# A decoder layer on one core: ScalarE multiplies the probabilities of 22 head pairs with the reciprocal sums, row by row, in place of VectorE and GpSimd

## The chip, the cores and the metric

The kernel runs on one core of a Trainium2 chip. A core has five engines with queues of their own: TensorE (PE, matrix products; its weight loads are shown as PEld), VectorE (DVE), ScalarE (ACT), GpSimd (POOL) and SyncE (SP, which here only issues transfers). They meet at semaphores alone: an instruction waits until a counter has reached a value, and all that stands behind it in its engine's queue waits too. The metric is the device time of one execution in microseconds.

## The reference

One pre-norm decoder layer in float32 over x of 16 sequences x 128 tokens x 256 features, three blocks, each on a layer norm of x and added to x:

- attention with 16 heads of 128: Q, K, V = x̂ W + b; rotary embedding of Q and K; scores Q K^T / sqrt(128), causal mask; `probs = softmax(scores)`; `z = probs V`; `out = z W_O + b_O`. This is the block that the change touches: of the softmax it is the division by the row sum.
- a long convolution of 256 features with filters of 128 taps, gated by a context (`ctx_2048`).
- a mixture of experts, 16 experts of 176 with the best 4 a token, beside a shared expert of 704.

## The kernel before

**Tiling.** The 16 sequences are four groups (g = 0 to 3) of GB = 4, a group being 512 tokens. The 16 heads are PAIRS = 8 pairs. The attention is a loop over steps s = 8g + p, one for each pair p of a group, and three more to drain it. All five engines run this loop, each with its own order written out by hand. Step s works on several pairs at once: Q and K of pair p (of number s), V, scores, maxima and exponentials of number s - 1, the weighed values of number s - 2, and the output projection of number s - 3. `live(k)` says whether the pair k back exists. Weights are kept as two float32r parts (`_hi`, `_lo`), and a product is three matmuls (lines 594 to 596, 656 to 658).

**What runs beside the attention.** From g = 1 on, the steps also carry the convolution block of the group before: at p = 2 its layer norm (`cross_head`, line 1657), at p = 3 turned tokens and a skip term (`vcs`, `cross_skip`), from p = 4 on products `kv` on GpSimd (line 1475), matmuls with them on TensorE (lines 713 to 715) and multiplications and sums on VectorE (lines 1684, 1699). For g = 2 and 3 the routing of the group two back stands there as well: at p = 2 TensorE turns its tokens (`token_turn`, line 609), which ScalarE and VectorE split (`tokens_high`, `th`; `tl`).

**A pair's softmax.** For head h of the pair VectorE scales and masks the scores into `prob[h]` (line 1600) and takes the negated row maximum (1604). ScalarE takes the exponential, one ACTIVATE for each of the four sequences, with the row sum from its accumulator (1226). VectorE takes the reciprocal `rtotal` (1608). A multiplication of `prob[h]` by `rtotal` follows: for h = 0 on GpSimd (`first_probs`, 1412), for h = 1 on VectorE (`second_probs`, 1628), one instruction of 128 x 512 with the reciprocals broadcast.

**Two ways to turn the probabilities.** z needs them transposed. For pairs 8 to 29 (`by_dma`, 22 of 32) ScalarE copies `prob[h]` into two planes of 16-bit halves (`prob_planes`, 1214), SP stores them in DRAM (489) and a transposing DMA brings them back as `prob_t[h]` (494). The other pairs are transposed by TensorE (669). Then TensorE weighs the values (687), ScalarE adds the bias of V (`take_weighed`, 1259) and rounds to `z_hi` (1266), GpSimd makes `z_lo` (1407), and TensorE projects (892 to 896) one step later.

**What sets the order around the change.** ScalarE's step begins with the two halves of V (`take_values`, 1237, `v_taken`), which TensorE has projected into bank 1 and bank 4, then the planes of head 1; then, for each head, exponential, bias, `z_hi`; last the planes of head 0. TensorE uses bank 1 again once V has been taken from it: at p = 0 for the second half of the turned tokens of the next group (865), at p = 2 (g = 2 and 3) for `token_turn` right behind V's projection, otherwise behind the output projection. VectorE's step ends with four `turn` products of Q and K (1619) with the two reciprocals among them, then `second_probs`, then `rot` (1640) of Q and K; GpSimd does the other half of `rot` (1447). TensorE's scores (919) need all four.

Of the kernel before, what the change touches and what calls it, by code (L numbers as in the profile page):

```python
# [8 lines left out]
ACT = mybir.ActivationFunctionType  # L9
# [5 lines left out]
GB = 4  # L15
# [57 lines left out]
def by_dma(t):  # L73
    return PAIRS <= t < PAIRS * GROUPS - 2


def dma_before(t):
    return min(max(t - PAIRS, 0), PAIRS * (GROUPS - 1) - 2)
# [24 lines left out]
def decoder(nc, x_in, wqkv_in, bqk_in, bv_in, wo_in, bo_in, trig_in, mask_in, ident_in,  # L103
# [7 lines left out]
    with ExitStack() as ctx:  # L111
        def sb(name, shape, dt=F32, c=ctx):
            return c.enter_context(nc.sbuf_tensor(name, shape, dt))
# [4 lines left out]
        def sem(name):  # L118
            return ctx.enter_context(nc.semaphore(name))
# [67 lines left out]
        prob = [sb(f"prob{h}", [128, GB, SEQ], c=tctx) for h in range(2)]  # L187
# [11 lines left out]
        rtotal = sb("rtotal", [128, 2, GB], c=tctx)  # L199
# [110 lines left out]
        rtotal_ready = sem("rtotal_ready")  # L310
        prob_ready = [sem(f"prob_ready{h}") for h in range(2)]
# [88 lines left out]
        def value_order(g, p, live):  # L400
            late = live(1) and live(2) and (p in (1, 2) or (g == 0 and p > 2)) and not by_dma(g * PAIRS + p - 2)
            return (1, 0) if late else (0, 1)
# [735 lines left out]
        def _(act):  # L1138
            def split_hi(n):
                act.wait_ge(raw_loaded[n % 2], 16 * (n // 2 + 1))  # L1140
                p = n // CH
                if p >= WRING and n % CH == 0:
                    act.wait_ge(w_stored[W_AT[p]], 64 * W_NTH[p])
                    act.wait_ge(v_ready, 2 * (p - WRING) + 2)
                nc.scalar.copy(w_hi[:, W_AT[p], n % CH, :], raw[n % 2][:]).then_inc(w_hi_done, 1)
# [18 lines left out]
            def root(lo, hi):  # L1164
                k = roots[0]
                roots[0] += 1
                act.wait_ge(var_ready, 2 * k + 2)
                nc.scalar.activation(rstd[:, lo:hi], newton[:, lo:hi], ACT.Sqrt).then_inc(rstd_ready, 1)
# [41 lines left out]
            def prob_planes(t, h):  # L1210
                act.wait_ge(prob_ready[h], t + 1)
                if dma_before(t):
                    act.wait_ge(prob_stored, 16 * (2 * dma_before(t) + h - 1))
                nc.scalar.copy(planes[h][:], prob[h][:].bitcast(U16).rearrange("p b (k i) -> p b i k", i=2)).then_inc(planes_ready, 1)

            root(0, GB)
            split_hi(0)
            split_hi(1)

            def step(g, p, live, first):  # L1220
                s = g * PAIRS + p
# [9 lines left out]
                order = value_order(g, p, live)  # L1231

                def take_values(half):
                    act.wait_ge(v_ready, s * 2 - 1 + order.index(half))
                    if live(3):
                        act.wait_ge(zt_ready, s * 2 - 4)
                    nc.scalar.copy(v[(p - 1) % 2][:, 2 * half:2 * half + 2, :],
                                   v_bank[half][:].rearrange("p (b n) -> p b n", b=2)).then_inc(v_taken, 1)

                if live(1):  # L1240
                    take_values(order[0])
                    if order == (0, 1):
                        take_values(1)
                if by_dma(s - 2):
                    prob_planes(s - 2, 1)
                if p == 0 and live(0):
                    for c in range(CH):
                        act.wait_ge(xt_ready, g * 2 + c + 1)
                        nc.scalar.copy(xt_hi[:, c, :], proj[c][:]).then_inc(xt_hi_done, 1)
# [25 lines left out]
                elif live(2):  # L1275
                    for i in range(4):
                        h = i % 2
# [26 lines left out]
                if live(1) and not by_dma(s - 2):  # L1304
                    exps(0)
                    exps(1)
                if by_dma(s - 1):
                    prob_planes(s - 1, 0)
                if first and p < PAIRS - 1:
                    split_hi(2 * p + 2)  # L1310
# [6 lines left out]
                if p == 2 and 0 < g < GROUPS:  # L1317
                    root((g - 1) * GB, g * GB)

            attention(step)  # L1320


# [79 lines left out]
        def _(pool):  # L1402
# [7 lines left out]
            def first_probs(s):  # L1410
                pool.wait_ge(rtotal_ready, s * 2 - 1)
                nc.gpsimd.tensor_tensor(prob[0][:], prob[0][:],  # L1412
                                        rtotal[:, 0, :].unsqueeze(2).to_broadcast([128, GB, SEQ]),
                                        ALU.mult).then_inc(prob_ready[0], 1)
                pool.wait_ge(prob_ready[0], s)

            def core_step(g, p, live, first):
                s = g * PAIRS + p
                late = by_dma(s - 2)
                if live(2):  # L1420
                    z_low(s, 0)
                    if not late:
                        z_low(s, 1)
                if late:
                    first_probs(s)
                    z_low(s, 1)
                for m in range(2):
                    if live(0):
                        pool.wait_ge(qk_used, s * 4 + 2 * m + 2)
                        if live(1):  # L1430
                            pool.wait_ge(s_ready, s * 2)
                        pool_rot(m, s)
                    if m == 0 and live(1) and not late:
                        first_probs(s)
                if p == 1 and live(0):

                    pool.wait_ge(small_loaded, SMALL)
                    pool.wait_ge(xhat_ready, g * GB + GB)
                    xg = x[:, g * GB:(g + 1) * GB, :]
                    nc.gpsimd.tensor_tensor(xg, xg, bo[:].unsqueeze(1).to_broadcast([128, GB, D]),  # L1440
                                            ALU.add).then_inc(bo_added, 1)
                    pool.wait_ge(bo_added, g + 1)
# [46 lines left out]
            last = GROUPS - 1  # L1489
# [21 lines left out]
        def _(dve):  # L1511
# [61 lines left out]
            def step(g, p, live, first):  # L1573
                s = g * PAIRS + p
# [35 lines left out]
                for m in range(2):  # L1610
                    t = turn[m]
                    if live(0):
                        for i in range(2):

                            dve.wait_ge(qk_ready, s * 4 + 2 * m + i + 1)
                            if i == 0 and live(1):
                                dve.wait_ge(rot_pool, s * 2 - 1 + m)
                                dve.wait_ge(rot_dve, s * 2 - 1 + m)
                            last = nc.vector.scalar_tensor_tensor(  # L1619
                                turn_all[m][:, 2 * i:2 * i + 2, :], qk_bank[2 * m + i][:].unsqueeze(1).to_broadcast([128, 2, GT]),  # L1620
                                bqk[:, p, 2 * m + i:2 * m + i + 1],
                                trig[:].rearrange("p a b t -> p a (b t)"), ALU.add, ALU.mult)
# [3 lines left out]
                def second_probs():  # L1626
                    dve.wait_ge(rtotal_ready, s * 2)
                    nc.vector.tensor_tensor(prob[1][:], prob[1][:],
                                            rtotal[:, 1, :].unsqueeze(2).to_broadcast([128, GB, SEQ]),
                                            ALU.mult).then_inc(prob_ready[1], 1)  # L1630

                if by_dma(s - 1):
                    second_probs()
                for m in range(2):
                    t = turn[m]
                    if live(0):
# [316 lines left out]
            last = GROUPS - 1  # L1953
# [222 lines left out]
```

## Time and profile before

| | us |
|---|---|
| median of three runs | 947.0 (946.83 to 950.6) |
| the profiled execution, its own time | 949.05 |
| its span, from first to last instruction | 947.2 |
| TensorE busy | 900.5 (95%) |
| VectorE busy | 801.2 (85%) |
| ScalarE busy | 455.7 (48%) |
| GpSimd busy | 498.5 (53%) |

A row of waits names who waited, for whom, the total, how often and the longest. A row of a timeline has start and duration, engine, line, operation, output and input tiles, how many were merged, and in brackets the idle time before it and who ended it. Matmuls overlap, so the durations of neighbours don't add. PEclk is TensorE's granted clock as a share of full speed.

### The profile page before, as it was taken

The numbers are of one execution on the slowest core, as the hardware profiler recorded it, in microseconds if no ns is written. First come the engines' busy times: TensorE is split into PE (matmuls) and PEld (weight loads), VectorE is DVE, ScalarE is ACT, GpSimd is POOL, SyncE is SP. The second block draws the span as 40 slices with busy tenths as digits, with TensorE's granted clock in tenths as the row PEclk, the third lists the DMA queues.
The fourth block names the chain that finished last, engine by engine and source line by source line (L and its number), as shares of the span: only waits on it lengthen the run. The fifth ranks groups of instructions, "written<-read, shape, count | busy, mean of one in ns | idle before, by whom it ended". The sixth has DMA issues, their size and how long they took to land.

```text
span 947.2 us, 19251 instructions
## 1 busy us (share of the span) xinstructions
PE 900.5 (95%) x6119; PEld 803.3 (85%) x6119; DVE 801.2 (85%) x1706; ACT 455.7 (48%) x1227; POOL 498.5 (53%) x380
## 2 busy tenths in 40 slices
PE   7899999999999989999998999989998999999996
PEld 6798888888899878898897888877887799999985
DVE  7988877988888989888897988966788888888867
ACT  3657655554445554444664433562155344445430
POOL 1533434465563435777362677625717377777760
PEclk9999999999999999999998999999999999999998
DMA  8795381665445654655788666425255377787879
GB/s 279 274 352 215 129 308 48 177 183 197 134 143 167 212 171 134 186 172 182 225 266 270 206 197 182 138 84 217 72 199 165 79 131 128 128 132 127 130 123 302
DMA packets 137489, 169.59 MB, mean 179 GB/s; under 512 B 54960, under 2 KB 112176, under 8 KB 136112
## 3 DMA queue, kind: packets, MB, share of 16 engines
q1 hardware_dynamic: 122944, 149.31, 48.9%
q0 software_dynamic: 14448, 19.05, 12.4%
q8 instruction: 53, 0.87, 0.4%
q14 instruction: 44, 0.36, 0.1%
HBM read 100.52 MB, written 58.44 MB: 168 GB/s over the span
## 4 chain that ended last, share of the span: by engine, by line
PE 68%; DVE 15%; issue 6%; POOL 5%; DMA 3%; ACT 2%; SPq 1%; DVEq 0%; POOLq 0%
PE bank L656 5%; PE bank L658 5%; PE bank L657 5%; PE bank L687 5%; PE bank L919 5%; PE bank L594 5%; PE bank L596 4%; PE bank L595 4%; PE bank L1032 4%; DVE rot L1640 3%; PE bank L713 3%; DVE turn L1619 3%; PE bank L714 3%; PE bank L715 3%; POOL xs L1454 2%
## 5 line engine op out<-in xcount | busy, mean ns | idle before, releaser
L1619 DVE SCALAR_TENSOR_TENSOR turn<-bank,bqk,trig 128x1024 f32<-128x1024 f32 x128 | 162.4, 1279 | 30.9 <-PE bank L658 28.9
L1407 POOL TENSOR_TENSOR z_lo<-prob_t,z_hi 128x512 fp32r<-128x512 f32 x64 | 83.5, 1304 | 199.0 <-ACT z_hi L1266 197.9
L1226 ACT ACTIVATE prob<-prob,negmax 128x128 f32<-128x128 f32 x256 | 99.4, 390 | 124.2 <-DVE negmax L1604 124.1
L1506 POOL DMA_INDIRECT sums<-ysb,token_at x79 | 123.3, 1560 | 56.8 <-DMA sums<-ysb,token_at 28.2
L1447 POOL TENSOR_TENSOR rot<-turn 128x512 f32<-128x512 f32 x64 | 95.4, 1490 | 42.5 <-DVE turn L1619 30.3
L656 PE MATMUL bank<-xt_hi,w_hi 128*128 128x512 f32 x256 | 109.6, 428 | 6.2 <-DVE vcs L1674 4.1
L658 PE MATMUL bank<-xt_hi,w_lo 128*128 128x512 f32 x256 | 101.9, 398 | 0.0
L657 PE MATMUL bank<-xt_lo,w_hi 128*128 128x512 f32 x256 | 101.4, 396 | 0.0
L1454 POOL DMA_INDIRECT xs<-xh,dest x64 | 71.4, 1115 | 43.0 <-DVE dest L1787 25.2
L1640 DVE TENSOR_TENSOR rot<-turn 128x512 f32<-128x512 f32 x64 | 93.0, 1493 | 0.0
L1475 POOL TENSOR_TENSOR kv<-c_t,v_t 128x512 f32<-128x512 f32 x60 | 71.8, 1224 | 19.2 <-ACT v_t L1188 12.2
L687 PEld LDWEIGHTS bank<-prob_t,v 128*128 128x128 f32 x512 | 66.2, 193 | 13.1 <-issue 6.3
L892 PE MATMUL bank<-wo_hi,z_hi 128*128 128x256 f32 x256 | 73.7, 288 | 3.6 <-issue 3.6
L594 PE MATMUL bank<-w_hi,xt_hi 128*128 128x256 f32 x256 | 73.6, 288 | 2.2 <-DVE turn L1619 2.1
L687 PE MATMUL bank<-prob_t,v 128*128 128x128 f32 x512 | 68.5, 277 | 6.6 <-ACT prob_t L1259 4.2
L894 PE MATMUL bank<-wo_lo,z_hi 128*128 128x256 f32 x256 | 73.1, 285 | 0.0
L896 PE MATMUL bank<-wo_hi,z_lo 128*128 128x256 f32 x256 | 73.1, 285 | 0.0
L596 PE MATMUL bank<-w_hi,xt_lo 128*128 128x256 f32 x256 | 72.4, 283 | 0.0
L595 PE MATMUL bank<-w_lo,xt_hi 128*128 128x256 f32 x256 | 72.4, 283 | 0.0
L919 PE MATMUL bank<-rot 64*128 64x128 f32 x1024 | 65.8, 278 | 2.6 <-DVE rot L1640 2.6
L919 PEld LDWEIGHTS bank<-rot 64*128 64x128 f32 x1024 | 59.6, 188 | 9.9 <-issue 5.6
L1412 POOL TENSOR_TENSOR prob<-prob,rtotal 128x512 f32<-128x512 f32 x32 | 33.3, 1041 | 59.2 <-DVE rtotal L1608 58.5
(202 smaller groups left out, 2563.7 us busy)
## 6 DMA issues: line engine op xcount, KB each, us to landing
w_hi<-w_dram SPq DMA_DIRECT2D x24, 768.0 KB, 5.1
w_lo<-w_dram SPq DMA_DIRECT2D x24, 768.0 KB, 6.3
prob_dram<-planes SPq DMA_DIRECT2D x44, 256.0 KB, 2.4
xe_all<-xs SPq DMA_DIRECT2D x79, 132.5 KB, 2.7
wo_hi<-wo_dram SPq DMA_DIRECT2D x26, 256.0 KB, 6.5
wo_lo<-wo_dram SPq DMA_DIRECT2D x26, 256.0 KB, 7.2
sums<-zeros SPq DMA_DIRECT2D x3, 2176.0 KB, 13.1
raw<-in_wqkv SPq DMA_DIRECT2D x16, 384.0 KB, 4.4
```

What stands on the lines that cost most here:

```text
L594: nc.tensor.matmul(o, lh, rh, start=(i == 0), stop=False)
L595: nc.tensor.matmul(o, lh, rl, start=False, stop=False)
L596: last = nc.tensor.matmul(o, ll, rh, start=False, stop=(i == n - 1))
L656: nc.tensor.matmul(o, hi, xt_hi[:, c, :], start=(c == 0), stop=False)
L657: nc.tensor.matmul(o, hi, xt_lo[:, c, :], start=False, stop=False)
L658: last = nc.tensor.matmul(o, lo, xt_hi[:, c, :], start=False, stop=(c == CH - 1))
L687: last = nc.tensor.matmul(zt_bank[:, b * 128:(b + 1) * 128], v[p % 2][:, b, h * DH:(h + 1) * DH], prob_t[h][:, b, :], start=True, stop=True)
L919: last = nc.tensor.matmul(score[h][:, t], rot[0][i][rows, t], rot[1][i][rows, t], start=(i == 0), stop=(i == 1))
L1226: last = nc.scalar.activation(prob[h][:, b, :], prob[h][:, b, :], ACT.Exp, bias=negmax[:, h, b:b + 1], accum_out=total[:, h, b:b + 1])
L1506: nc.gpsimd.indirect_dma_start(sums_dram[s % SUMS], bass.IndirectOffsetOnAxis(ap=token_at[:, s:s + 1], axis=0), ysb[s % YBUFS][:], None, c ...
L1619: last = nc.vector.scalar_tensor_tensor(turn_all[m][:, 2 * i:2 * i + 2, :], qk_bank[2 * m + i][:].unsqueeze(1).to_broadcast([128, 2, GT]), ...
L1640: nc.vector.tensor_tensor(rot[m][0][:], t[0], t[3], ALU.subtract).then_inc(rot_dve, 1)
```

## The change

In steps whose pair goes by DMA, ScalarE gets `weigh_probs(t, h)`: it waits for the reciprocal of pair t and head h and multiplies `prob[h]` in place, one ACTIVATE of 128 x 128 for each of the four sequences, the reciprocal of a row as its per-partition scale. For head 1 it stands at the start of the step after next, ahead of V's halves; for head 0 at the end of the next step, ahead of its planes. `second_probs` and `first_probs` are no longer called for these pairs. At the step's start the order on ScalarE becomes: product of head 1, V of bank 1, planes of head 1, V of bank 4 (before: both halves of V, then the planes). The other ten pairs are as before. Lines behind 1215 move by 7 to 10.

```diff
+            def weigh_probs(t, h):
+                act.wait_ge(rtotal_ready, 2 * t + h + 1)
+                for b in range(GB):
+                    last = nc.scalar.activation(prob[h][:, b, :], prob[h][:, b, :], ACT.Copy,
+                                                scale=rtotal[:, h, b:b + 1])
+                last.then_inc(prob_ready[h], 1)
...
+                if by_dma(s - 2):
+                    weigh_probs(s - 2, 1)
                 if live(1):
                     take_values(order[0])
-                    if order == (0, 1):
-                        take_values(1)
                 if by_dma(s - 2):
                     prob_planes(s - 2, 1)
+                if live(1) and order == (0, 1):
+                    take_values(1)
...
                 if by_dma(s - 1):
+                    weigh_probs(s - 1, 0)
                     prob_planes(s - 1, 0)
...
                 if late:
-                    first_probs(s)
+                    if not by_dma(s - 1):
+                        first_probs(s)
                     z_low(s, 1)
...
-                    if m == 0 and live(1) and not late:
+                    if m == 0 and live(1) and not late and not by_dma(s - 1):
                         first_probs(s)
...
-                if by_dma(s - 1):
-                    second_probs()
```

ScalarE's queue where step 17 (g = 2, p = 1) ends and step 18 begins, before; `bank1` and `bank4` hold the projected V:

```order
L1266 CAST z_hi1<-prob_t1 128x512
L1214 COPY planes0<-prob0 128x1024
L1237 COPY v1<-bank1 128x512
L1237 COPY v1<-bank4 128x512
L1214 COPY planes1<-prob1 128x1024
```

The same place after; `th_early` is the copy of the routed tokens that TensorE turned:

```order
L1275 CAST z_hi1<-prob_t1 128x512
L1219 ACTIVATE prob0<-prob0,rtotal 128x128 x4
L1214 COPY planes0<-prob0 128x1024
L1219 ACTIVATE prob1<-prob1,rtotal 128x128 x4
L1244 COPY v1<-bank1 128x512
L1214 COPY planes1<-prob1 128x1024
L1244 COPY v1<-bank4 128x512
L1201 CAST th_early<-bank0 128x512
```

Four ACTIVATEs now stand ahead of the planes of head 0 and four ahead of V of bank 1, and V of bank 4 has moved behind the planes of head 1.

GpSimd's queue in a step with `kv` products, before:

```order
L1407 TENSOR_TENSOR z_lo0<-prob_t0,z_hi0 128x512
L1412 TENSOR_TENSOR prob0<-prob0,rtotal 128x512
L1407 TENSOR_TENSOR z_lo1<-prob_t1,z_hi1 128x512
L1447 TENSOR_TENSOR rot01<-turn0 128x512
L1447 TENSOR_TENSOR rot11<-turn1 128x512
L1475 TENSOR_TENSOR kv0<-c_t,v_t 128x512
```

And after:

```order
L1417 TENSOR_TENSOR z_lo0<-prob_t0,z_hi0 128x512
L1417 TENSOR_TENSOR z_lo1<-prob_t1,z_hi1 128x512
L1458 TENSOR_TENSOR rot01<-turn0 128x512
L1458 TENSOR_TENSOR rot11<-turn1 128x512
L1486 TENSOR_TENSOR kv0<-c_t,v_t 128x512
```

The product, with its wait for the reciprocal, is gone from between the two `z_lo`. VectorE's queue loses line 1628 between the last reciprocal and `rot` in the same way; TensorE's and SP's queues are unchanged.

## Rows read from the trace of the kernel before

**Rows 1.** The page, engine busy us (share of the span) xinstructions

```profile
PE 900.5 (95%) x6119; PEld 803.3 (85%) x6119; DVE 801.2 (85%) x1706; ACT 455.7 (48%) x1227; POOL 498.5 (53%) x380
```

**Rows 2.** Waits of TensorE, 156:606: us in total, times, longest

```profile
PE bank L656 <- DVE vcs L1674: 4.1, 2, 3.1
PE bank L687 <- ACT prob_t L1259: 2.5, 2, 1.7
PE bank L687 <- DMA prob_t<-prob_dram: 2.4, 2, 1.8
PE bank L713 <- POOL kv L1475: 1.9, 3, 0.8
PE bank L919 <- DVE rot L1640: 1.4, 2, 0.9
PE bank L703 <- DVE vcs L1669: 0.8, 3, 0.3
PE bank L713 <- DVE zc L1684: 0.4, 1, 0.4
```

**Rows 3.** Groups, 160:592: shapes xcount | busy us, mean ns | idle before

```profile
L1226 ACT ACTIVATE prob<-prob,negmax 128x128 f32<-128x128 f32 x176 | 68.4, 390 | 121.7 <-DVE negmax L1604 121.7
...
L1628 DVE TENSOR_TENSOR prob<-prob,rtotal 128x512 f32<-128x512 f32 x22 | 34.8, 1581 | 0.7
...
L1259 ACT ACTIVATE prob_t<-bank,bv 128x512 f32<-128x512 f32 x42 | 28.5, 677 | 26.4 <-PE bank L687 26.3
...
L1412 POOL TENSOR_TENSOR prob<-prob,rtotal 128x512 f32<-128x512 f32 x22 | 22.9, 1041 | 52.3 <-DVE rtotal L1608 52.2
```

**Rows 4.** Timeline of VectorE, 334 to 341: start us, us, operation

```profile
335.30 1.80 DVE L1628 TENSOR_TENSOR prob<-prob,rtotal 128x512 f32<-128x512 f32 x1
337.02 2.38 DVE L1640 TENSOR_TENSOR rot<-turn 128x512 f32<-128x512 f32 x2
```

**Rows 5.** Timeline of GpSimd, 331 to 341 us

```profile
334.00 1.30 POOL L1407 TENSOR_TENSOR z_lo<-prob_t,z_hi 128x512 fp32r<-128x512 f32 x1 [0.66 <-ACT z_hi L1266]
335.25 3.01 POOL L1447 TENSOR_TENSOR rot<-turn 128x512 f32<-128x512 f32 x2
```

**Rows 6.** Timeline of ScalarE, 316 to 321.5 us

```profile
316.13 0.62 ACT L1266 CAST z_hi<-prob_t 128x512 fp32r<-128x512 f32 x1
316.66 1.04 ACT L1214 COPY planes<-prob 128x1024 uint16<-128x1024 uint16 x1
317.61 0.58 ACT L1237 COPY v<-bank 128x512 f32<-128x512 f32 x1
```

**Rows 7.** Timeline of ScalarE, 419 to 426 us

```profile
420.70 1.05 ACT L1214 COPY planes<-prob 128x1024 uint16<-128x1024 uint16 x1 [2.56 <-POOL prob L1412]
422.33 0.59 ACT L1237 COPY v<-bank 128x512 f32<-128x512 f32 x1 [0.58 <-PE bank L596]
...
424.26 1.05 ACT L1214 COPY planes<-prob 128x1024 uint16<-128x1024 uint16 x1
```

**Rows 8.** Timeline of TensorE, 426 to 427.5 us

```profile
426.64 0.67 PE L713 MATMUL bank<-kv,toep 128*128 128x256 f32 x2
```

**Rows 9.** Timeline of VectorE at 317 and at 422 us, line 1608

```profile
317.23 0.17 DVE L1608 RECIPROCAL rtotal<-total 128x4 f32<-128x4 f32 x1
...
422.10 0.17 DVE L1608 RECIPROCAL rtotal<-total 128x4 f32<-128x4 f32 x1
```

**Rows 10.** Timeline of TensorE, 318.6 to 320 us

```profile
318.70 1.03 PE L609 MATMUL bank<-ident,xh 128*128 128x128 f32 x8
```

**Rows 11.** Timeline of ScalarE and TensorE, 283 to 286 us

```profile
283.14 0.59 ACT L1237 COPY v<-bank 128x512 f32<-128x512 f32 x1 [0.58 <-PE bank L596]
...
284.38 1.04 PE L865 MATMUL bank<-ident,xhat 128*128 128x128 f32 x8
```

**Rows 12.** Windows: busy us of each engine, PEclk, DMA share, GB/s

```profile
313.50:318.70 5.20, 5.20 (x38) 4.93 (x39) 5.16 (x8) 4.65 (x13) 4.09 (x4) 1.00 0.32 121
...
351.50:354.90 3.40, 3.40 (x11) 2.68 (x10) 1.45 (x3) 0.70 (x4) 1.62 (x2) 0.51 0.02 7
```

## The prediction

> **What bounds the kernel now.** I read the busy table first [rows 1]: TensorE is busy 900.5 of 947.2 us. The change touches steps 9 to 31 (step s = 8g + p), about 160 to 606 us. A busy TensorE row is no proof that it sets the end, so I read next what TensorE waited for in this stretch [rows 2]. The seven sums make 4.1 + 2.5 + 2.4 + 1.9 + 1.4 + 0.8 + 0.4 = 13.5 us in 450. That is the prize: 4.1 + 1.4 + 0.8 + 0.4 = 6.7 us end with VectorE, 1.9 with GpSimd, 2.5 with ScalarE (its exponentials start behind VectorE's maxima), 2.4 with a transposing DMA. Everywhere else TensorE is gapless and an engine made faster frees nothing. So the question is small on both sides: which of these 15 waits shrink, and where a longer ScalarE queue opens a new one.
>
> **What leaves.** 22 products on VectorE and 22 on GpSimd [rows 3]: 34.8 and 22.9 us of engine time. Their worth is not that. Step 17's end shows how VectorE's product lies [rows 4]: it takes 1.80 us at 335.30, the two rotations 2.38 behind it. GpSimd's rotations start at 335.25 and take 3.01 together [rows 5]. The recorded 1.80 is mostly waiting: the pattern is GpSimd, VectorE, GpSimd, VectorE, one holding the other off (I put VectorE's own share at about 0.7 a product: three VectorE and two GpSimd products fill the 4.1 us from 335.25 to 339.40, at 0.7 and 1.0 each). Without the product VectorE's first rotation takes its slot, GpSimd's second goes next, VectorE's second last: 0.6 us saved, not 1.8. The Trainium skill (SBUF — State Buffer, "SBUF: two separate sides") calls this an exclusive lock between GpSimd and a VectorE instruction with two SBUF inputs, where the loser blocks for the whole instruction. By that rule the chain gives back 0.6 us here; by the recorded durations it would be 1.8. The rows agree with the rule.
>
> Where GpSimd's z_lo still holds the lock as VectorE gets free, or GpSimd is done earlier (all steps with kv products), VectorE gets the first slot and 1.4 to 1.7 us are saved. In these steps only small waits stand, each under 1 us, and all go: rot 1.4 (steps 10, 11), kv 1.9 (steps 12, 21, 29), zc 0.4 (step 20), and one vcs wait of 0.26, together **−3.9 us**. GpSimd's share goes for a second reason: its product stood between the two z_lo and waited for a reciprocal, so z_lo of head 1, both rotations and the kv products all move up by at least 1.04 us [rows 3], more than the longest kv wait, 0.8.
>
> The four long waits at p = 1 and p = 3 (313.5 and 472.4 behind prob_t; 350.3 and 509.2 behind vcs) end chains of VectorE that start behind the rotations of p = 0 and p = 2. Each chain moves up by 0.6, or by 1.7 if VectorE wins the first slot, which in rows 4 and 5 it loses by 50 ns. I take 0.6 for each: **−2.4 us** (bounds 0, and −5.5 when each is capped by its wait). After it the same VectorE instructions are late next.
>
> **What is added.** Eight ACTIVATEs a pair on ScalarE, four 128x128 for a head. No row shows this operation. From above: the exponential of the same tile takes 390 ns [rows 3] and its successors follow at that distance, 4 x 0.39 = 1.56 us. From below: a cast of 128x512 takes 620 ns and starts 0.1 us before its predecessor's end, and the planes copy of 1024 elements takes 1.04 [rows 6], so 128 more elements cost 0.1 us and one of 128 takes 0.3, or 0.2 net of overlap: 4 x 0.2 = 0.8. A per-partition operand costs 0.1 (677 with a bias operand [rows 3] against 580 for the v copy [rows 6], both from PSUM). I take 0.3 each, **1.3 us a head**, 22 x 2 x 1.3 = 57 us of ScalarE time. No table load joins: Copy stands beside Exp and Sqrt in before too. Nearly all of it is off the path: per step ScalarE waits several us for VectorE's maxima (121.7 us in the stretch [rows 3]).
>
> In an ordinary step head 0's planes start at 420.70, behind GpSimd's product of 1.04 [rows 7]; ScalarE's takes 1.3 in its place, 0.3 more. Head 1's product starts behind the reciprocal, at 422.3 [rows 9], and ends at 423.6; V of bank 1 is taken at 424.1 instead of 422.9, head 1's planes end at about 425.1 (before, 425.3 [rows 7]). What waits behind it is V of bank 4, now behind the planes: 1.2 later. TensorE needs bank 1 only behind the output projection, at 426.6 [rows 8]; slack 2.5, cost nothing. If it were gone the cost would be the excess, per step. The stores and transposing DMAs of SP move by under 1.5 us with the planes of head 0 and not with those of head 1; the two waits for them in this stretch stand behind the 2.2 MB fills of the sums, which move only slightly, so I count 0.
>
> **Where it is not hidden: p = 2 of g = 2 and 3 (steps 18 and 26).** There TensorE turns the routed tokens at once behind V's projection, into the bank whose V ScalarE must have taken. Before: z_hi ends at 316.75, planes run to 317.70, V is taken at 318.19 [rows 6], TensorE starts its turn at 318.70 [rows 10] without waiting. After, ScalarE has no pause: z_hi ends 316.75, product of head 0 to 318.0, planes to 319.1, product of head 1 (its reciprocal is there since 317.4 [rows 9]) to 320.3, V to 320.8. TensorE starts at 320.8: **+2.1 us, twice, +4.2** (at 0.8 a head +1.1 each, at 1.56 a head +2.6 each). ScalarE's queue and TensorE are tied by the same exponentials before it, so nothing absorbs it; in step 19 the VectorE chain starts behind TensorE's last projection and moves along.
>
> **p = 0 (steps 16, 24).** Before, V is taken by 283.73 and the turn of the next group's tokens starts at 284.38, its second bank at 284.9 [rows 11]. After, V is there at 285.0 to 285.3, and the xt_hi copies end 0.6 to 0.9 later, where VectorE's faster rotations no longer stand in xt_lo's way: **+0.5 us** for both.
>
> **The clock.** Behind the wait of 3.1 us TensorE is granted half speed for 3.4 us (PEclk 0.51), that is 1.2 for 2.4 GHz; behind the wait of 1.7, which ends at 313.5, it is not (1.00) [rows 12]. Half speed for 3.4 us costs 1.7. A new wait of 2.1 us lies between, a wait of 3.1 becomes 2.5. I count 0 and keep ±1.7, twice for the new waits.
>
> **Sum.** −3.9 − 2.4 + 4.2 + 0.5 = −1.6. The profiled execution took 949.05 us (span 947.2), so 947.4 after; the median of the runs is 2.05 lower, 947.0, which gives **945.4 us**.
>
> **Rivals.**
> *A: the late V decides.* One mechanism: the products cost 1.56 a head, so TensorE waits 2.6 us in steps 18 and 26, long enough that the clock falls behind each (2 x 1.7). −3.9 − 0 (chains of p = 1 stand, since the root of p = 1 comes later behind the longer queue) + 5.2 + 3.4 + 1.0 = +5.7, 952.7 us. It decides from about 1.5 us a head. For it: exponential's distance of 0.39; against: that one has an accumulator read beside it. The Trainium skill (ScalarE: Activation LUTs, "Rules for kernel authors") says that multiplications belong on VectorE, not ScalarE, which speaks against this change; by that rule it comes out on A's side, and the trace of before can't show it.
> *B: VectorE wins its slots.* The chains move by 1.7 and the 3.1 us wait falls to 1.4 without a clock drop: −3.9 − 5.5 − 1.7 + 4.2 + 0.5 = −6.4, 940.6 us. For it: 50 ns decide. Against: both engines are released by the same events as before.
> *C: the waits only change their name*, since the waits for VectorE and GpSimd come back as waits for PSUM banks or the sums' DMA: −3.9 and −2.4 halve, +1.5, 948.5 us.
>
> **Chances.** Forecast 0.52, A 0.17, B 0.15, C 0.16. This kernel's measurement can't tell less than 0.5% (4.7 us: 942.3 to 951.7) from no change. Faster takes nearly all of B and a little of the forecast, 0.18; slower takes most of A, 0.15; same 0.67. The range runs from B's time to just short of A's: 940.5 to 951.5.
>
> **What would show it.** The new ACTIVATEs near 0.3 us apart; a TensorE wait of about 2 us before the token turn in steps 18 and 26, put down to ScalarE's v; no waits for kv, rot or zc; the vcs waits 0.6 shorter; idle before ScalarE's exponentials down by about 2 us a step. Wrong it is if TensorE waits for v in ordinary steps too, or if the rotations end 1.7 earlier at p = 0 and p = 2.

## The result

The changed kernel takes 944.7 us (median of 20 runs, 938.3 to 951.2) beside 949.9 us for the kernel before, measured again beside it (20 runs, 946.0 to 954.4). The ratio is 0.9954 with a 95% interval of 0.9939 to 0.9969: 4.4 us less (2.9 to 5.8; the two medians lie 5.2 apart). The forecast was 945.4 us, 1.6 less than before. That this stands so near to 944.7 is luck: it was counted from 947.0, the median of three runs of the kernel before, whose 20 runs have 949.9. The sign and the class hold, but the gain is nearly three times the forecast, and the ledger below shows that several terms were wrong in both directions. The profiled execution took 946.15 us (949.05 before).

The busy line of the page [rows 1]:

```profile
PE 895.0 (95%) x6119; PEld 800.8 (85%) x6119; DVE 754.6 (80%) x1684; ACT 507.3 (54%) x1403; POOL 473.3 (50%) x358
```

VectorE is relieved of 46.6 us and GpSimd of 25.2, and ScalarE has 51.6 more, yet TensorE's, for the same 6119 instructions, moves by 5.5, and about half of that is only less time at half clock in this execution (22.5 us in place of 27.7). The waits of TensorE in 156 to 606 us [rows 2]:

```profile
PE bank L687 <- DMA prob_t<-prob_dram: 7.4, 3, 3.4
PE bank L609 <- issue: 3.8, 2, 1.9
PE bank L656 <- DVE vcs L1683: 2.9, 1, 2.9
PE bank L713 <- POOL kv L1486: 2.1, 3, 1.5
PE bank L703 <- DVE vcs L1678: 0.3, 1, 0.3
```

The waits for `rot`, `zc` and ScalarE's `prob_t` are gone. In their place stand the token turn (two of 1.9) and a larger DMA wait, and the sum is 16.5 us where it was 13.5. The kernel is faster all the same, so this view alone doesn't explain it.

The groups of the stretch 160 to 592 us by shape [rows 3]:

```profile
L1233 ACT ACTIVATE prob<-prob,negmax 128x128 f32<-128x128 f32 x178 | 69.2, 390 | 109.8 <-DVE negmax L1615 109.8
...
L1219 ACT ACTIVATE prob<-prob,rtotal 128x128 f32<-128x128 f32 x176 | 56.3, 390 | 20.8 <-DVE rtotal L1619 20.7
...
L1649 DVE TENSOR_TENSOR rot<-turn 128x512 f32<-128x512 f32 x44 | 54.1, 1270 | 0.0
```

The product on ScalarE has the duration of the exponential of the same tile, 390 ns, but four take 1.28 us, as the timelines below show, so they stand 0.30 apart. The busy time of 56.3 us is the 57 that were foreseen. ScalarE's idle time ahead of its exponentials fell only from 121.7 to 109.8 us, 0.5 a step where 2 were foreseen: 20.8 us of new idle time lie ahead of the products.

### Three places in the two traces

**The rotations at p = 2, step 18** [rows 4, 5]. VectorE before, around the rows named:

```profile
335.10 0.17 DVE L1608 RECIPROCAL rtotal<-total 128x4 f32<-128x4 f32 x1
...
339.33 0.15 DVE L1545 TENSOR_TENSOR newton<-rstd 128x4 f32<-128x4 f32 x1
```

After, VectorE, then GpSimd, then ScalarE, 331 to 338 us:

```profile
332.92 0.17 DVE L1619 RECIPROCAL rtotal<-total 128x4 f32<-128x4 f32 x1
333.01 2.36 DVE L1649 TENSOR_TENSOR rot<-turn 128x512 f32<-128x512 f32 x2
335.50 1.04 DVE L1556 TENSOR_TENSOR newton<-rstd 128x4 f32<-128x4 f32 x1
...
333.02 3.51 POOL L1458 TENSOR_TENSOR rot<-turn 128x512 f32<-128x512 f32 x2
...
333.97 1.28 ACT L1168 ACT_TABLE_LOAD   x1
335.26 0.20 ACT L1168 ACTIVATE rstd<-newton 128x4 f32<-128x4 f32 x1
```

Before, GpSimd's rotation started first, by 50 ns. Now VectorE's does, by 13 ns: it begins 0.08 us before the reciprocal ahead of it has ended, since it has no wait, where the product had to wait for that reciprocal and started behind its end. Its first rotation takes the slot. From the reciprocal's start to the end of VectorE's last rotation it is 2.45 us, where it was 4.31 (335.10 to 339.41): 1.86 less and not 0.6. That is rival B's mechanism. It holds for VectorE's queue alone: GpSimd now ends last, at 336.53, 3.61 us behind the reciprocal, so all four rotations are there only 0.70 earlier. And step 19 gets little of it. The Newton step behind waits for ScalarE's root (335.26, behind the product, the planes and a table load), and then its first instruction, of 4 elements a partition, takes 1.04 us, where it took 0.15 before; GpSimd's second rotation runs until 336.53. That instruction ends 3.62 us behind the reciprocal, where it was 4.38: of the 1.86 us the chain to step 19 keeps 0.76.

**Behind V in step 18** [rows 6, 10]. ScalarE 312 to 317, then TensorE:

```profile
312.40 1.28 ACT L1219 ACTIVATE prob<-prob,rtotal 128x128 f32<-128x128 f32 x4
313.71 1.05 ACT L1214 COPY planes<-prob 128x1024 uint16<-128x1024 uint16 x1
314.66 1.27 ACT L1219 ACTIVATE prob<-prob,rtotal 128x128 f32<-128x128 f32 x4
315.84 0.56 ACT L1244 COPY v<-bank 128x512 f32<-128x512 f32 x1
...
316.51 1.06 PE L609 MATMUL bank<-ident,xh 128*128 128x128 f32 x8 [1.92 <-issue]
```

This is the chain that the forecast worked out: product, planes, product, V, then the turn. TensorE waits 1.92 us, where 2.1 were foreseen. The releaser is called "issue", and that it is V follows from the start times (V is taken by 316.40) and from the run in which V is taken first (below).

**The first convolution product, step 13.** GpSimd and TensorE before:

```profile
244.59 2.88 POOL L1475 TENSOR_TENSOR kv<-c_t,v_t 128x512 f32<-128x512 f32 x2
...
245.83 0.28 PE L896 MATMUL bank<-wo_hi,z_lo 128*128 128x256 f32 x1
246.14 0.67 PE L713 MATMUL bank<-kv,toep 128*128 128x256 f32 x2
```

and after:

```profile
241.74 3.46 POOL L1486 TENSOR_TENSOR kv<-c_t,v_t 128x512 f32<-128x512 f32 x3
...
244.00 0.28 PE L896 MATMUL bank<-wo_hi,z_lo 128*128 128x256 f32 x1
244.12 0.59 PE L713 MATMUL bank<-kv,toep 128*128 128x256 f32 x2
```

The start before the convolution's own start is 0.31 us away before, and 0.12 after, which is the pace of all its neighbours. So TensorE was waiting for `kv0` (which ended at 245.99; after, at 243.15), but the wait lay under the modelled end of the last matmul and no view of waits names it. Each of the steps 13 to 15, 22 and 23 gains 0.25 us, 0.18 of it at this start. [Rows 8] show such a start (426.64), and the forecast took it for one that waits for nothing.

### The profile page after: what moved, and what is told of

It reads as the page before. It is cut to its first block, busy times and chain, and to the rows that moved or that the text cites. A ratio compares the mean times of both kernels' runs of the same rounds, so it can differ in the third digit from the quotient of the medians.

```text
span 944.3 us, 19361 instructions
## 1 busy us (share of the span) xinstructions
PE 895.0 (95%) x6119; PEld 800.8 (85%) x6119; DVE 754.6 (80%) x1684; ACT 507.3 (54%) x1403; POOL 473.3 (50%) x358
## 4 chain that ended last, share of the span: by engine, by line
PE 73%; DVE 8%; DMA 6%; ACT 5%; issue 4%; POOL 4%; SPq 0%; DVEq 0%; POOLq 0%; ACTq 0%
PE bank L594 5%; PE bank L687 5%; PE bank L919 5%; PE bank L596 5%; PE bank L595 5%; PE bank L656 5%; PE bank L658 5%; PE bank L657 4%; PE bank L1032 4%; DMA prob_dram<-planes 3%; PE bank L713 3%; PE bank L714 3%; PE bank L715 3%; PE bank L990 3%; PE bank L892 2%
## 5 line engine op out<-in xcount | busy, mean ns | idle before, releaser
L1458 POOL TENSOR_TENSOR rot<-turn 128x512 f32<-128x512 f32 x64 | 99.3, 1552 | 59.8 <-DVE turn L1630 31.5
L1465 POOL DMA_INDIRECT xs<-xh,dest x64 | 71.4, 1115 | 43.0 <-DVE dest L1796 25.2
L1693 DVE TENSOR_TENSOR zc<-bank,c_t 128x512 f32<-128x512 f32 x64 | 44.0, 687 | 51.8 <-PE bank L715 48.9
L1649 DVE TENSOR_TENSOR rot<-turn 128x512 f32<-128x512 f32 x64 | 78.7, 1271 | 0.0
L892 PE MATMUL bank<-wo_hi,z_hi 128*128 128x256 f32 x256 | 73.6, 288 | 3.6 <-issue 3.6
L1486 POOL TENSOR_TENSOR kv<-c_t,v_t 128x512 f32<-128x512 f32 x60 | 65.5, 1119 | 20.3 <-ACT v_t L1188 12.0
L594 PE MATMUL bank<-w_hi,xt_hi 128*128 128x256 f32 x256 | 73.6, 287 | 2.1 <-DVE turn L1630 2.0
L894 PE MATMUL bank<-wo_lo,z_hi 128*128 128x256 f32 x256 | 73.1, 286 | 0.0
L896 PE MATMUL bank<-wo_hi,z_lo 128*128 128x256 f32 x256 | 73.1, 285 | 0.0
L1219 ACT ACTIVATE prob<-prob,rtotal 128x128 f32<-128x128 f32 x176 | 56.3, 390 | 20.8 <-DVE rtotal L1619 20.7
```

Of the source, the lines that this page charges most:

```text
L594: nc.tensor.matmul(o, lh, rh, start=(i == 0), stop=False)
L1458: nc.gpsimd.tensor_tensor(rot[m][1][:], turn[m][1], turn[m][2], ALU.add).then_inc(rot_pool, 1)
```

## The experiments

Every experiment is a whole kernel. Two were timed (fills_after_timed, both_moves); of the others there is one profiled execution each, and its whole time says little: the kernel before ranges from 944.7 to 954.4 us, and what stands behind step 32's scores, where no edit changes anything, takes 329 to 339 us in these executions, half of the time at half clock taken off. So the stretches ahead of it are compared. The table gives the time between the starts of the score products (the first with `rot`) of two steps, with half of the time at half clock taken off, so that the clock's luck isn't in it (half speed for a time t costs t/2). "Half clock" is that time in steps 9 to 32. fills_after and fills_after_timed are one program, as are the two kernels and their repeats.

| kernel | 9-12 | 12-16 | 16-20 | 20-25 | sum 9-25 | 25-29 | 29-32 | half clock |
|---|---|---|---|---|---|---|---|---|
| before | 54.2 | 83.0 | 73.6 | 99.7 | 310.5 | 79.3 | 61.7 | 10.2 |
| before_again | 54.2 | 82.9 | 73.4 | 99.8 | 310.3 | 81.3 | 61.7 | 6.8 |
| after | 52.9 | 82.2 | 73.1 | 97.5 | 305.5 | 85.5 | 61.2 | 6.8 |
| after_again | 52.9 | 82.2 | 72.5 | 97.5 | 305.1 | 80.5 | 61.2 | 20.5 |
| slot_lost | 53.0 | 82.2 | 74.3 | 99.7 | 309.2 | 79.2 | 62.8 | 13.7 |
| v_first | 52.9 | 82.2 | 71.1 | 99.9 | 306.0 | 82.0 | 62.5 | 10.2 |
| head1_only | 53.6 | 82.9 | 71.4 | 99.1 | 307.1 | 82.5 | 61.7 | 10.2 |
| head0_only | 54.1 | 82.0 | 74.5 | 97.9 | 308.5 | 83.0 | 61.8 | 6.8 |
| order_only | 54.2 | 82.9 | 73.7 | 99.7 | 310.5 | 84.3 | 61.7 | 6.8 |
| fills_before | 54.2 | 82.9 | 73.1 | 100.1 | 310.3 | 79.1 | 61.7 | 13.7 |
| fills_after | 52.9 | 82.2 | 73.4 | 98.9 | 307.4 | 78.7 | 62.9 | 0.0 |
| fills_after_timed | 52.8 | 82.2 | 73.4 | 97.5 | 305.9 | 78.5 | 61.2 | 3.4 |
| both_moves | 52.9 | 82.2 | 71.2 | 99.1 | 305.4 | 76.3 | 63.0 | 3.4 |

### slot_lost: VectorE's rotation waits for the reciprocal again

Changed kernel with
```diff
+                        if m == 0 and by_dma(s - 1):
+                            dve.wait_ge(rtotal_ready, s * 2)
                         nc.vector.tensor_tensor(rot[m][0][:], t[0], t[3], ALU.subtract)
```


> The changed kernel, where VectorE's first rotation waits for its own last reciprocal again, as the product did before. Theory S (in steps 16 and 18 VectorE's rotation wins the first slot against GpSimd's by 14 ns only because that wait is gone): GpSimd's rotation goes first, VectorE's two end about 1.2 us later in these steps and in 24 and 26, and a wait of TensorE for prob_t at p = 1 of 0.5 to 1.2 us is back, 0.5 to 1.2 us lost at each. Theory R (the chain is shorter by the removed product itself): the wait of some 0.1 us costs 0.1 us, no wait comes back.

One execution: 955.1 us (before on the same chip: 954.3). VectorE and GpSimd in step 18, 337 to 341 us:

```profile
337.26 0.17 DVE L1619 RECIPROCAL rtotal<-total 128x4 f32<-128x4 f32 x1
337.56 3.33 DVE L1651 TENSOR_TENSOR rot<-turn 128x512 f32<-128x512 f32 x2
...
337.36 2.99 POOL L1458 TENSOR_TENSOR rot<-turn 128x512 f32<-128x512 f32 x2
```

GpSimd goes first again, and from the reciprocal's start to the last rotation's end it is 3.63 us: 0.68 less than before, which is the term of 0.6, and 1.18 more than after. So both sizes of the forecast were right, and only the choice between them was wrong. The end of all four rotations is not moved (3.63 for 3.61 us), so what the slot decides is VectorE's own chain. A wait of 1.0 for `prob_t` at p = 1 (step 17) is back, and steps 16 to 20 take 1.2 and 1.8 us more than in the two executions of the changed kernel. At step 25, where the expectation wanted the same, no wait came back. The 2.2 us more in steps 20 to 25 are for the most part a wait for `zc` (1.8) at p = 6. v_first has one there as well (1.1), though its rotations have their slot, and fills_after, in which no product or order is changed, is 1.4 us slower in these steps than the same program in fills_after_timed. So they need not be the slot's, and their cause stays open.

### v_first: V ahead of the product in steps 18 and 26

Changed kernel with
```diff
-                if by_dma(s - 2):
+                if by_dma(s - 2) and not turns_next(s):
                     weigh_probs(s - 2, 1)
                 if live(1):
                     take_values(order[0])
+                if by_dma(s - 2) and turns_next(s):
+                    weigh_probs(s - 2, 1)
```
where `turns_next(s)` is true for steps 18 and 26; in the steps ahead of them (17 and 25) head 0's product is left to GpSimd too.

> The changed kernel, where ahead of the two token turns (steps 18 and 26) the product of head 0 stays on GpSimd and ScalarE takes V of bank 1 before the product of head 1. If the 1.9 us waits before the token turn are ScalarE's late V, both are gone. By theory 1 the first is kept (step 25's scores 1.5 to 2 us earlier than in the changed kernel) and the second is given back at the prob_t waits behind the fills: step 29's scores within 0.5 us of the changed kernel's. Rival: both are kept, 3.5 us by step 29.

One execution: 952.9 us. Both waits ahead of the token turn are gone, and steps 16 to 20 take 71.1 in place of 72.5 to 73.1: the 1.9 us wait was V's, and 1.4 to 2.0 of it come back. Then 2.4 are lost in steps 20 to 25 and 1.3 in 29 to 32, in waits for `zc` and for "issue" that this run has and the two executions of the changed kernel don't, so that step 25's scores come no earlier than there (306.0 us for 305.5 and 305.1), against the expectation. Whether V's place causes these waits isn't shown: fills_after has such waits too, in an execution that takes V where the changed kernel does.

### head1_only and head0_only: one half of the change

head1_only moves VectorE's products alone, head0_only GpSimd's alone, both with the new order of V and planes:
```diff
+                if by_dma(s - 2):
+                    weigh_probs(s - 2, 1)
...
-                if by_dma(s - 1):
-                    second_probs()
```


> Only VectorE's product (head 1) goes to ScalarE, GpSimd keeps head 0's. From step 9's scores to step 25's the changed kernel is 5.0 us ahead of the kernel before. If the parts act where the rows put them: the rot waits of steps 10 and 11 (1.4) and the prob_t wait of step 17 (1.7) go, the kv waits and the 0.25 us a step ahead of the first kv matmul stay (3 us less than the changed kernel), and the wait before the token turn is 0.8, not 1.9. So 2.5 to 3.5 us ahead. Rival (GpSimd's rotations and kv are held by VectorE's product alone): the kv waits go here too, 5 us or more ahead.

```diff
                 if by_dma(s - 1):
+                    weigh_probs(s - 1, 0)
                     prob_planes(s - 1, 0)
...
-                    first_probs(s)
+                    if not by_dma(s - 1):
+                        first_probs(s)
```


> Only GpSimd's product (head 0) goes to ScalarE, VectorE keeps head 1's, and ScalarE takes V of bank 1 with no product ahead of it. The kv waits and the 0.25 us a step go (2 to 2.9 us by step 25), the prob_t wait of step 17 and the rot wait of step 11 stay, and the wait before the token turn is 0.9. So 1 to 2.5 us ahead of the kernel before at step 25's scores. Rival (the lead comes from VectorE alone): 0.

One execution each: 953.2 and 950.5 us, before 950.0 (median of 13). TensorE's waits of head0_only in 156 to 606 us:

```profile
...
PE bank L687 <- ACT prob_t L1266: 2.4, 2, 1.6
PE bank L609 <- issue: 1.5, 2, 0.7
PE bank L919 <- DVE rot L1649: 1.3, 2, 0.9
PE bank L713 <- POOL kv L1484: 0.9, 2, 0.6
...
```

The waits for `rot` and `prob_t` belong to VectorE's product: they stay here and are gone in head1_only. The gain of steps 12 to 16 (0.8 us, the unnamed wait for `kv0`) belongs to GpSimd's: head0_only has it (82.0) and head1_only has not (82.9). In the token turn head 0's product alone costs 0.7 us, head 1's alone 0.6 and 0.4, both together 1.9. In steps 9 to 25 the halves give 3.4 (310.5 to 307.1) and 2.0, as foreseen (2.5 to 3.5, and 1 to 2.5), together 5.4 for the 5.0 to 5.4 of the whole: to the spread of single executions they add.

### order_only: V of bank 4 behind the planes, no product moved

```diff
                 if live(1):
                     take_values(order[0])
-                    if order == (0, 1):
-                        take_values(1)
                 if by_dma(s - 2):
                     prob_planes(s - 2, 1)
+                if live(1) and order == (0, 1):
+                    take_values(1)
```


> The kernel before with only the new order at the step's start: V of bank 1, planes of head 1, V of bank 4. TensorE needs bank 4 late in every step, so steps 9 to 25 take the same as before to 0.3 us. Rival: V of bank 4 waits with the planes for VectorE's product and delays the routed tokens' copies at p = 2, 0.5 us or more lost at each of steps 18 and 26.

One execution: 955.3 us. Steps 9 to 25 are those of before to 0.1 us, so the order by itself costs nothing, as foreseen. Steps 25 to 29 lose 5.0, with DMA waits of 1.0, 1.6 and 3.4. This kernel has no lead that it could give back, and so it speaks against the reading "the lead is given back at the DMA".

### before_again and after_again: the same kernels once more

> The kernel before, unchanged, in one more profiled execution. The question: how far do the stretches between two steps' scores differ between executions of one and the same kernel? Theory (the differences are the kernels'): steps 9 to 25 within 0.5 us of the first execution's 312.2 (with the same half-clock time, 3.4 us), steps 25 to 29 within 1 us of its 82.7 once half of the half-clock time is taken off (79.3), the same DMA waits in steps 25 to 29 (0.7 and 1.8). Rival (steps 25 to 29 are luck of the DMA queues and of the clock): steps 25 to 29 come out 2 us or more away, with other DMA waits, so that the 84.3 to 85.5 of the kernels with a changed order say little.

> The changed kernel, unchanged, in one more profiled execution. Theory (the differences are the kernels'): steps 9 to 25 within 0.5 us of 307.2 (half-clock time 3.4), steps 25 to 29 about 85.5 after half of the half-clock time is off, with three waits for the transposing DMA of 1.3, 2.6 and 3.4 us; the two waits ahead of the token turn 1.9 each. Rival (luck of the queues): the token-turn waits and steps 9 to 25 repeat, but steps 25 to 29 come out 2 us or more away, with other DMA waits.

One execution each: 950.1 and 949.5 us. TensorE's waits of after_again in 156 to 606 us:

```profile
PE bank L687 <- DMA prob_t<-prob_dram: 4.1, 2, 2.3
PE bank L609 <- issue: 3.8, 2, 1.9
PE bank L656 <- DVE vcs L1683: 3.8, 2, 2.9
PE bank L713 <- POOL kv L1486: 0.8, 3, 0.4
...
```

Steps 9 to 25 repeat within 0.4 us, and so do the token turn's two waits and `vcs` in step 19. Steps 25 to 29 don't: 85.5 and 80.5 us with one kernel, 79.3 and 81.3 with the other. The DMA waits are 7.4 against 4.1, the 1.5 for `kv` (GpSimd then waited for the load of `c_t`) doesn't come again. In both pairs the expectation's theory holds for steps 9 to 25 and its rival for steps 25 to 29: there a difference of up to 5 us comes without any change of the kernel. The half clock differs as much: 6.8 and 20.5 us. But 0.4 us is not the whole spread of steps 9 to 25. fills_after and fills_after_timed, one program, differ by 1.5 there (307.4 and 305.9) and by 1.7 in steps 29 to 32. TensorE's waits of fills_after in 156 to 606 us that fills_after_timed doesn't have:

```profile
PE bank L714 <- issue: 1.3, 2, 0.6
...
PE bank L657 <- DVE zc L1694: 0.5, 2, 0.3
```

So a single execution with waits for `zc` or "issue" of this size doesn't show that its edit caused them.

### fills_before and fills_after: the three fills issued in step 8

```diff
-                    if g == GROUPS - 1 and 0 < p <= SUMS:
-                        rows = sums_dram[p - 1].rearrange("(n p) d -> p n d", p=128)
-                        sp.dma_start(rows, zeros...)
+                    if g == 1 and p == 0:
+                        for i in range(SUMS):
+                            rows = sums_dram[i].rearrange("(n p) d -> p n d", p=128)
+                            sp.dma_start(rows, zeros...)
```


> The kernel before, with the three 2.2 MB fills of the sums issued at g = 1, p = 0 and no longer at g = 3, p = 1 to 3. Theory 1 (the fills hold back the stores of the planes in steps 26 to 29, and the changed kernel gives its lead back there): the two waits of TensorE for prob_t from the DMA (2.4 us) go, the vcs wait of step 27 stays at about 1 us, and step 29's scores start 1.5 to 3 us earlier against step 25's. Theory 2 (steps 26 to 29 are set by VectorE's and TensorE's own work and the clock, the DMA waits only change their name): under 0.7 us.

> The changed kernel with the same move of the fills. Theory 1: the prob_t waits of 1.3, 2.6 and 3.4 us and the kv wait of 1.5 us in group 3 go; the lead over the fills_before kernel is about 5 us at step 25's scores and still 3 to 5 us at step 29's, where the pair with the fills in place had 5.2 and 0.8. The time is 5 to 7 us below the changed kernel. Theory 2: the lead shrinks to about 1 us by step 29 here too, by the wait before the token turn and the clock.

> The changed kernel with the three fills of the expert sums issued together in step 8 (g = 1, p = 0) in place of one each in steps 25, 26 and 27; timed now, since a single look gave 943.66 us with no half clock until the end. Theory (the fills cost the changed kernel what its DMA waits and the clock behind them show, 7.4 and 1.7 us): 939 to 941 us, ratio to before about 0.990 to 0.992, like the kernel with both moves (0.9905), of which the V of bank 1 taken earlier is then worth 0 to 2 us. Rival (the fills are hidden as they are and the single look was the clock alone): 943 to 945 us, ratio 0.994 to 0.996, like the changed kernel itself (0.9954), and the gain of both moves comes from V taken earlier.

Single executions gave 954.2 us on the kernel before (954.3 without the move) and 943.7 on the changed one. Timed (6 executions, 11 of before), the changed kernel with this move takes 940.1 us beside 948.9: ratio 0.9904, interval 0.9866 to 0.9943. The transfers in 462 to 530 us, issue, count, KB each, median us to landing, first of after, then of fills_after_timed:

```profile
sums<-zeros SPq DMA_DIRECT2D x3, 2176.0 KB, 13.4
...
prob_dram<-planes SPq DMA_DIRECT2D x6, 256.0 KB, 5.8
```

```profile
prob_dram<-planes SPq DMA_DIRECT2D x6, 256.0 KB, 2.3
```

and the waits of fills_after_timed in 156 to 606 us:

```profile
PE bank L657 <- DVE vcs L1684: 5.9, 2, 3.0
PE bank L610 <- issue: 3.8, 2, 1.9
PE bank L688 <- ACT prob_t L1269: 0.9, 1, 0.9
PE bank L714 <- POOL kv L1487: 0.8, 3, 0.4
...
```

Each fill takes about 13 us to land, and the planes stored next behind it take 7.4, 9.2 and 10.3 us in after, 7.6, 8.3 and 8.0 in after_again and 6.4, 10.2 and 7.5 in before, where all others but one (4.1, in after) take 2.4 or 2.5; the median of 5.8 depends on which stores the stretch holds. Without the fills no DMA wait is left. In part the wait for `vcs` in step 27 takes the place, 3.0 us. In the kernel before it does so too (3.1), and steps 25 to 29 take 79.1 us without the fills there, 79.3 and 81.3 with them: by the first pair the move brings nothing, as the second theory has it, by the second 2.2 us, and it was not timed. The lead of fills_after over fills_before is 2.9 us at step 25's scores and 3.3 at step 29's, where 5 and 3 to 5 were expected.

Not all of the timed gain is in the waits. The runs list the mean granted clock of each: 0.9877 over the 20 of the changed kernel and 0.991 over the 6 with the fills moved. At full speed the one would save 11.6 us of its time and the other 8.3, so some 3.3 of the 4.6 us between 944.7 and 940.1 come with the clock, as far as 6 executions tell.

### both_moves: fills_after with v_first

> The changed kernel with the three fills at g = 1, p = 0, and with V of bank 1 taken ahead of the product before the two token turns (the product of head 0 on GpSimd there). With the fills out of the way the 1.9 us of both token turns are kept: step 29's scores 3 to 4 us before those of the kernel with only the fills moved, counted from step 9 and apart from the half-speed stretches of TensorE. Time against the kernel before: ratio 0.985 to 0.992. Rival (other waits take the place): no better than the fills alone, 0.990 to 0.994.

939.2 us beside 950.0, ratio 0.9905, interval 0.9871 to 0.9938, with a few waits for `zc` and "issue". That is the ratio of the moved fills alone (0.9904), as the rival has it. Taking V first gives 2.2 us in each of the two stretches around the token turn (71.2 for 73.4, 76.3 for 78.5), and step 29's scores come 2.7 us before those of fills_after_timed, where 3 to 4 were foreseen. Beside fills_after_timed it loses 1.6 and 1.8 behind them, beside fills_after 0.2 and 0.1, so that the loss is V's isn't shown. Both versions are faster than the kernel before. They were not timed beside the changed kernel, whose interval (0.9939 to 0.9969) theirs just touch. The simpler one is as good.

## Why the forecast was right in class and short in size

In steps 9 to 25 the two executions of either kernel agree within 0.4 us, so there the ledger can be held against the forecast. The times are steps in the distance between the same matmul of before and of after:

| term in steps 9 to 25 | forecast | measured |
|---|---|---|
| small waits of steps 10 to 12 (rot, kv, vcs) | -1.9 | -1.3 |
| ordinary steps 13 to 15, 22, 23 | 0 | -1.3 |
| p = 0, step 16 | +0.25 | 0.0 |
| `prob_t` wait at 313.5 | -0.6 | -1.8 |
| token turn | +2.1 | +2.1 |
| `vcs` in step 19, both waits | -0.6 | -0.7 |
| `zc` and `kv` in steps 20 and 21 | -1.3 | -1.5 |
| rest, in pieces below 0.2 | | -0.5 |
| sum | -2.05 | -5.0 |

- **The product on ScalarE, 0.3 us each: right.** Four take 1.28 us (1.3 foreseen; bounds 0.8 and 1.56). Rival A needed 1.5 and did not come.
- **The new waits at the token turn, 2.1 each: right** (1.92 and 1.91). Ordinary steps don't wait for V, as foreseen, and p = 0 doesn't either (0.0 for 0.25).
- **"Without the product VectorE's first rotation takes its slot, GpSimd's second goes next ... 0.6 us saved": the failed step.** The queue that loses by 50 ns was taken from rows in which VectorE's first instruction had a wait. Without it, that instruction starts 0.08 us before its predecessor's end and wins by 13 ns: VectorE's last rotation ends 1.86 us earlier (slot_lost: 0.68 with the wait), which is one of the two signs by which the forecast was to be called wrong. This is B's mechanism, to which I gave 0.15 with the argument that both engines are released by the same events. They are, but the wait itself cost the start. It pays 1.8 for the foreseen 0.6 at the `prob_t` wait of step 17. (The rows called "step 17's end" are step 18's, at p = 2; step 16 shows the same pattern, 4.31 and 2.45 us.)
- **"Each chain moves up" for `vcs` at p = 3: right in size by luck.** 0.7 were measured for 0.6, but the rotations end 1.86 earlier, and of this 0.76 is left behind the first Newton instruction. The chain has a second leg, ScalarE's root, which stands behind the new product and a table load, and its next VectorE instruction takes 1.04 us beside GpSimd. The wait itself, foreseen 0.6 shorter, stays at 2.9 (3.1 before), since TensorE comes earlier too.
- **The bound of -5.5 for the four chains: an error in the sum.** With 1.7 each, capped by the waits of 1.7, 0.8, 3.1 and 1.0, it is -5.2, and B's time 940.9.
- **"Ordinary steps: cost nothing": no cost, but a gain that I had not counted.** 0.25 us a step with the hidden wait for `kv0`; in steps 30 and 31 it is there as well.
- **"I count 0" for the DMAs: open in size.** The waits were 2.4 before, 4.3 in its repeat, 7.4 and 4.1 after. The two executions of one kernel lie up to 3.3 apart, so a cost of the change there can't be told from luck; that TensorE now arrives earlier at transfers whose time is set by the queue makes one plausible, and it was not shown.
- **The clock, 0 with 1.7 to either side: a term put too low, and too narrow a bound.** It was 6.8 us of half speed in one execution and 20.5 in the other, 6.9 us in time. The runs' mean granted clock is 0.9877 over the 20 of the changed kernel and 0.9902 over the 24 of the kernel before that stand beside the two later timings: 11.6 and 9.2 us lost, 2.4 us more (about 0.8 either way). These 24 ran at other times than the 20. The two waits at the token turn alone don't explain it: fills_after_timed has both and lists 0.991.
- **"No waits for kv, rot or zc": kv wrong.** 0.4 and 0.2 remain at p = 4 (steps 12 and 20), and the 0.26 for `vcs` in step 11 remains too. In step 12 GpSimd's rotations ahead of `kv` end 1.3 us earlier (203.2 to 202.0), since VectorE's go first, and TensorE is there 1.6 earlier.

The whole: 5.0 less in steps 9 to 25, and 0.5 in 29 to 32. Steps 25 to 29 ought to give some 0.5 (79.1 in fills_before, 78.6 in the two runs of after with moved fills). That makes 6.0. The runs say 4.4 (2.9 to 5.8). The 2.4 us that the changed kernel's runs lose more to the clock are of the size of the 1.6 that is missing; what the DMA waits and the rest of the kernel take or give beside it, single profiles can't resolve.

## What to carry to other kernels

Before "it loses the slot by 50 ns" is taken as fixed, ask whether the instruction that starts there has a wait on a semaphore and the one that takes its place has not. A start of a matmul that lags its neighbours' pace is a wait even where no view names it: compare start distances, not ends. Profile both kernels twice before explaining a stretch, above all where it holds large transfers on the queue that the critical ones use. And read the granted clock of all timed runs, not only of the profiled one: here its mean differs by 2.4 us' worth, where one execution can differ by 6.9.

## What the runs showed of the hardware

**Which of two engines goes first is decided by hundredths of a microsecond and costs whole instructions.** The same two rotations on VectorE take 2.36 us with the first slot and 3.33 without, and GpSimd's take 3.51 and 2.99. Even a product of 4 elements a partition took 1.04 us beside GpSimd's rotation; the same operation in slot_lost, where GpSimd was done, took 0.15:

```profile
340.82 0.15 DVE L1556 TENSOR_TENSOR newton<-rstd 128x4 f32<-128x4 f32 x1
```

**ScalarE's products.** 390 ns each with starts 0.30 apart. The Trainium skill (ScalarE: Activation LUTs, "What ACT_TABLE_LOAD costs") gives 280 ns and 0.833 a column with one per-partition operand, and an overlap of 93 ns between neighbours. For 128 columns that is an estimate of 387 ns and starts 0.29 apart; these rows agree. Its rule to use VectorE for multiplications ("Rules for kernel authors") would have spoken against the change; here no wait for ScalarE's products was found but in two steps, and the change gained.

**The same wait, with and without the lower clock.** Windows of 3.4 us behind the wait of 1.92 at the token turn, PEclk in the third column from the end, after:

```profile
316.60:320.00 3.40, 3.40 (x30) 3.40 (x31) 1.29 (x2) 2.21 (x4) 3.04 (x2) 1.00 0.55 140
```

and after_again:

```profile
317.70:321.10 3.40, 3.40 (x19) 3.40 (x18) 1.29 (x2) 1.62 (x4) 2.41 (x2) 0.51 0.63 154
```

The instructions and the wait (1.92 and 1.91) are the same, and TensorE runs at 2.4 GHz in the one and at 1.2 GHz in the other, which costs 1.7 us. So one profile doesn't tell whether a wait of 2 us brings it.
